# Attention beside a mixture of experts: tags in one load, and a tile's up-weight pieces split in two places

## The chip, the cores and the metric

One core of a Trainium2 chip runs the whole program in one launch. The metric is the time of an execution on the device in microseconds; lower is better. Engines are called TensorE (PE in the profile, PEld for its weight loads), VectorE (DVE), ScalarE (ACT), GpSimd (POOL) and SyncE (SP, which here only issues transfers and waits). An ending q (DVEq, SPq) marks the instruction queue of an engine: register work, waits, and the issuing of transfers.

## What is computed

The inputs are 2 x 1024 rows of 512 numbers. After a layer norm the output is the sum of three parts:

```python
xn = _layernorm(x, axis=-1)
x = x + attention(xn) + experts(xn)        # both read the same xn

# attention: 16 heads of 32, rotary embedding over the heads, causal softmax, scaled by 512 ** -0.5, projection
# experts: 8 of them, the best 2 per row, their weights normalised to sum 1
gate_up = jnp.einsum('th,eoh->eto', x, w1)          # w1: 8 x 704 x 512
g, u = jnp.split(gate_up, 2, axis=-1)
act = jax.nn.silu(g) * u
expert_out = jnp.einsum('eti,ehi->eth', act, w2)    # w2: 8 x 512 x 352
out = jnp.einsum('eth,te->th', expert_out, combine)
```

## The kernel before

**Stages.** `project_qkv` (up to about 110 us) normalises the rows, projects them, chooses two experts for each row and writes to memory. `attend` runs 16 rounds, a pair of heads each, of about 19.5 us; meanwhile it sorts the rows by expert: `route` gives each (row, choice) a place, and POOL scatters the row there by an indirect transfer into `routed` (32 transfers, in rounds 0 to 8, counted by `scattered`). `experts`, from about 562 us on, first does the second half of the output projection (8 steps, `LATE`), and then works through `SLOT_TILES` = 39 tiles of 128 sorted rows, each belonging to one expert.

**A routed row** has 514 numbers: 512 of xn, then its tag: the row of the output to which it belongs (an integer in the bits of a float), and the weight of the choice. In `acc` the output is gathered, by an indirect transfer that adds.

**A tile i of `experts`** takes these steps, and most buffers are double (r = i % 2):
- ScalarE loads `rows` (L816), three tiles ahead. TensorE turns them (`turn_rows`, L932) into `turn_ps`. ScalarE rounds them to `rows_hi` (L822), VectorE takes the rest as `rows_lo` (L888): two numbers of reduced precision stand for one float.
- The up weights are split in the same way, in DK = 4 pieces of 128 x 704: ScalarE casts `w1_hi` (`up_weights_high`, L826), VectorE subtracts (`up_weights_low`, L895, `w1_lo`, called w_lo in the trace). `w1_done` counts the pieces.
- TensorE forms the products `up(i, r, j)` in two halves, j = 0 for g and j = 1 for u, 12 products each: for each of the four pieces hi x hi, hi x lo, lo x hi (L940, L941, L942).
- ScalarE takes the silu of g (`gated`, L851), VectorE multiplies by u (`hidden`, L911), TensorE turns that (`turn_hidden`, L950), VectorE copies it (`hidden_t`, L881, L882), and TensorE multiplies it by w2 (`down_product`, L958, six passes).
- ScalarE scales the result by the weight in the tag into `y` (L839). POOL adds `y` to `acc` by the row numbers in the tag (L802), after the accumulate before it has landed (`added`), since two tiles can hold the same row.

**The order on each engine** is written out by hand, one `tile` function each, and each engine works its queue in order:
- TensorE in tile i: down(i-2), up half 0 of i, turn_hidden(i-1), turn_rows(i+1), up half 1 of i. Before half 0 it waits for all four pieces of tile i.
- ScalarE in tile i: y(i-2), the front two casts of tile i+1, silu(i), rows_hi(i+1), the rear two casts of i+1, and the load of rows(i+3).
- VectorE in tile i: the front two subtractions of tile i+1, hidden_t(i-1), rows_lo(i+1), the rear two subtractions of i+1, hidden(i).
- POOL in tile i: waits until y(i) is there and the accumulate i-1 has landed; a small `carrier` instruction; the accumulate i; then the load of the tag of tile i+1 (`load_tag`, L792), one piece of 8 bytes per partition. `y`(i) waits for that tag (`tag_in`).

Each engine reads a tile's place in the ring of weights from memory into a register (`slot_at`, `value_load`, L739). `run_tiles` writes tiles 0 to 3 and the last one (for ScalarE the last three) with constant addresses; those between are a loop of two tiles each, with addresses in registers. SP keeps a ring of three experts' weights (2.1 MB each, L757 to L759): an expert's weights are overwritten once `y_read` shows that its last tile is through.

## Time and profile before

| | us |
|---|---|
| median of 3 runs | 934.96 |
| the 3 runs | 934.89, 943.35, 934.96 |
| the profiled execution: its time | 937.0 |
| its span, first to last instruction | 935.1 |
| TensorE busy in the span | 829.9 (89%) |
| VectorE busy | 515.4 (55%) |
| ScalarE busy | 395.0 (42%) |
| GpSimd busy | 272.6 (29%) |

Times in rows are microseconds from the first instruction of the profiled execution, unless they are marked ns. A row of the timeline is: start, length, engine, line, operation, what is written <- what is read, shape, count, and in brackets how long the engine stood idle before it and what released it. Rows of neighbouring instructions of one kind are merged: their count is behind the x, their length that of the group. A share of busy time says nothing about what bounds a stage; the rows below are taken from the stage that the change touches.

### The profile page before, as it was taken

What the parts mean: (1) busy time and instruction counts of PE and PEld (TensorE: products, weight loads), DVE (VectorE), ACT (ScalarE), POOL (GpSimd) and SP (SyncE); (2) the same over time, 40 slices, a digit from 0 to 9 for tenths busy, and PEclk for the clock granted to TensorE, in tenths of its full rate; (3) what the DMA queues carried; (4) which work ended last, traced back from release to release, by engine and by line L of the source; (5) the groups of instructions that cost most, each with busy time, mean ns of one, the idle gap of its engine ahead of it and who ended that gap; (6) DMA issues with size and microseconds to landing.
All of it is one profiled execution on the core that took longest, in us unless ns stands there. A gap on an engine that the chain in (4) does not pass through costs nothing. (4 is left out here: it accounts for less than half of the span.)

```text
span 935.1 us, 13836 instructions
## 1 busy us (share of the span) xinstructions
PE 829.9 (89%) x3973; PEld 561.9 (60%) x3974; DVE 515.4 (55%) x1334; ACT 395.0 (42%) x779; POOL 272.6 (29%) x352
## 2 busy tenths in 40 slices
PE   3889999289989999999999999798989889899990
PEld 3678988254545555555554444576767667677760
DVE  5983453584566666666674021664656546666640
ACT  3321221014545555555655400454545545455630
POOL 3781000405132342423331510032323323333330
PEclk9999999758899999999999999998999999999995
DMA  9386596867356576676730138434454453633336
GB/s 318 142 262 206 202 312 203 250 164 227 97 155 165 175 182 165 182 189 178 196 100 14 41 103 275 161 68 137 73 151 120 100 149 67 160 68 67 68 35 200
DMA packets 76717, 143.21 MB, mean 153 GB/s; under 512 B 12928, under 2 KB 26752, under 8 KB 76608
## 3 DMA queue, kind: packets, MB, share of 16 engines
q10 hardware_dynamic: 29056, 58.28, 22.7%
q1 hardware_dynamic: 38192, 65.68, 22.7%
q0 software_dynamic: 9424, 18.69, 9.9%
q8 instruction: 22, 0.36, 0.2%
q14 instruction: 23, 0.19, 0.1%
HBM read 81.21 MB, written 61.15 MB: 152 GB/s over the span
## 5 line engine op out<-in xcount | busy, mean ns | idle before, releaser
L1342 ACT ACTIVATE probs<-scores_t 128x512 f32<-128x512 f32 (+3 forms) x384 | 163.8, 492 | 148.0 <-PE scores_t L1469 136.1
L895 DVE TENSOR_TENSOR w_lo<-w,w_hi 128x704 fp32r<-128x704 f32 x156 | 131.6, 884 | 121.3 <-ACT w_hi L826 115.7
L1446 PE MATMUL maxima<-k_stack,q_stack 96*128 96x512 f32 (+3 forms) x384 | 142.4, 391 | 15.2 <-DMA q_stack<-qk_hi 9.1
L1489 PE MATMUL o_acc<-probs,v_ones 128*64 128x512 f32 (+3 forms) x768 | 149.1, 511 | 0.0
L1469 PE MATMUL scores_t<-q_stack,k_stack 98*128 98x512 f32 (+3 forms) x384 | 138.3, 385 | 7.3 <-DMA q_stack<-row_lo 5.2
L1376 DVE TENSOR_REDUCE mx<-maxima 128x1 f32<-128x512 f32 x128 | 88.2, 689 | 88.4 <-PE maxima L1446 88.2
L1372 DVE CUSTOM_DVE_ANT_0 masked_scores<-maxima,mask_m 128x128 f32<-128x128 f32 (+3 forms) x256 | 121.6, 485 | 24.2 <-PE maxima L1446 21.1
L958 PE MATMUL down<-w,hidden_t 128*128 (+1 forms) x234 | 114.8, 628 | 20.7 <-DVE hidden_t L882 20.7
L826 ACT CAST w_hi<-w 128x704 fp32r x156 | 114.0, 782 | 34.7 <-issue 33.5
L940 PE MATMUL gu<-w_hi,rows_hi 128*128 128x352 f32 x312 | 120.6, 386 | 5.3 <-DVE rows_lo L888 4.0
L1469 PEld LDWEIGHTS scores_t<-q_stack,k_stack 98*128 98x128 f32 x384 | 73.5, 194 | 69.3 <-issue 42.1
L941 PE MATMUL gu<-w_lo,rows_hi 128*128 128x352 f32 x312 | 101.8, 326 | 0.0
L942 PE MATMUL gu<-w_hi,rows_lo 128*128 128x352 f32 x312 | 101.5, 325 | 0.0
L1446 PEld LDWEIGHTS maxima<-k_stack,q_stack 96*128 96x128 f32 x384 | 77.4, 203 | 36.0 <-DVE mx L1376 10.0
L1287 POOL TENSOR_SCALAR_AFFINE_SELECT probs<-probs 128x256 f32<-128x256 f32 x120 | 48.4, 406 | 145.3 <-ACT probs L1342 143.5
L1489 PEld LDWEIGHTS o_acc<-probs,v_ones 128*64 128x64 f32 x768 | 47.7, 139 | 64.7 <-issue 39.6
L839 ACT ACTIVATE y<-down,tag 128x512 f32<-128x512 f32 x39 | 26.8, 688 | 140.9 <-DMA tag<-routed 90.2
L958 PEld LDWEIGHTS down<-w,hidden_t 128*128 128x128 f32 (+1 forms) x234 | 44.0, 199 | 66.9 <-issue 66.6
L801 POOL TENSOR_TENSOR carrier_y<-ident 128x1 f32<-128x1 f32 x39 | 7.3, 188 | 242.2 <-ACT y L839 242.2
L802 POOL DMA_INDIRECT acc<-y,tag x39 | 63.9, 1639 | 16.9 <-issue 16.9
L940 PEld LDWEIGHTS gu<-w_hi,rows_hi 128*128 128x128 f32 x312 | 59.4, 190 | 15.6 <-DVE w_lo L895 6.3
L941 PEld LDWEIGHTS gu<-w_lo,rows_hi 128*128 128x128 f32 x312 | 59.5, 191 | 9.2 <-issue 9.2
(158 smaller groups left out, 1175.7 us busy)
## 6 DMA issues: line engine op xcount, KB each, us to landing
w<-in_w_t SPq DMA_DIRECT2D x8, 1408.0 KB, 6.4
routed<-blank_row ACTq DMA_DIRECT2D x20, 514.0 KB, 7.2
rows<-routed ACTq DMA_DIRECT2D x39, 256.0 KB, 3.6
qk_hi<-st_hi SPq DMA_DIRECT2D x32, 256.0 KB, 4.7
qk_lo<-st_lo SPq DMA_DIRECT2D x32, 256.0 KB, 6.1
q_stack<-qk_hi ACTq DMA_DIRECT2D x32, 256.0 KB, 4.0
k_stack<-qk_hi ACTq DMA_DIRECT2D x26, 256.0 KB, 4.7
v_all<-o_t SPq DMA_DIRECT2D x4, 1536.0 KB, 5.7
```

What stands on the lines that cost most here:

```text
L826: nc.scalar.copy(w1_hi[r][:, k, :], w1_rows(slot, k)).then_inc(w1_hi_done, 1)
L895: nc.vector.tensor_tensor(w1_lo[r][:, k, :], w1_rows(slot, k), as_f32(w1_hi[r][:, k, :]), ALU.subtract).then_inc(w1_done, 1)
L940: nc.tensor.matmul(out, hi, w1_hi[r][:, k, cols], start=(k == 0), stop=False)
L941: nc.tensor.matmul(out, hi, w1_lo[r][:, k, cols], start=False, stop=False)
L942: last = nc.tensor.matmul(out, lo, w1_hi[r][:, k, cols], start=False, stop=(k == DK - 1))
L958: last = nc.tensor.matmul(down[r][:], hidden_t[r][0:n, k, :], w2[0:n, bass.ds(e, 1), k, :].rearrange("p o n -> p (o n)"), start=(k == 0), ...
L1342: nc.scalar.activation(probs[:, k % PR, h, 0:w], scores_t[e % RING][:, 0:w], ACT.Exp).then_inc(exp_done, 1)
L1372: nc.vector.tensor_tensor_reduce(out=masked_scores[bank][:, 0:w], in0=scores, in1=mask_m[:, CH - w:CH], scale=1.0, scalar=NEG, op0=ALU.add ...
L1376: nc.vector.tensor_reduce(to, scores, AX.X, ALU.max).then_inc(m_free, 1)
L1446: nc.tensor.matmul(mb[at % RING][:, 0:w], q_st[i][0:3 * HD, h, t * P:(t + 1) * P], k_st[i][0:3 * HD, h, c * CH:c * CH + w], start=True, st ...
L1469: last = nc.tensor.matmul(out[:, 0:w], k_st[i][0:STACK, h, j * P:(j + 1) * P], q_st[i][0:STACK, h, t0:t0 + w], start=True, stop=not diag)
L1489: last = nc.tensor.matmul(o_acc[c][2 * HD * h:2 * HD * (h + 1), CH - w:CH], v_st[i][:, j, h:h + 2, :].rearrange("p o d -> p (o d)"), probs ...
```

## The change

The tags of all 39 tiles are loaded by one transfer, issued by SP in round 9 of `attend` into a tile `tags` that lives through the program (39 x 2 numbers per partition, so 4,992 pieces of 8 bytes). SP waits for `scattered` before it. `load_tag`, `tag_in` and the carrier instruction go; POOL copies the row numbers of the next tile into `row_index`, by an instruction in the place of the carrier, since the indirect transfer takes its addresses from there. In `experts` the split of the up weights moves: ScalarE casts the front two pieces of tile i+1 behind rows_hi(i+1), and the rear two as the first thing in tile i+1. VectorE subtracts all four pieces of tile i as the first thing in tile i. TensorE waits for each piece on its own within half 0. In the projection steps ahead of tile 0, its casts, its subtractions and its announcement each move one step up.

```diff
@@ -695,9 +695,9 @@
         hidden = [m.sbuf(f"hidden{r}", [P, I], F32) for r in range(2)]
         hidden_t = [m.sbuf(f"hidden_t{r}", [P, len(I_TILES), P], F32) for r in range(2)]
         y = m.sbuf("y", [P, 2, D], F32)
-        tag = m.sbuf("tag", [P, 2, XW - D], F32)
+        tags = keep["tags"]
         warm = m.sbuf("warm", [P, 1], F32)
-        carrier = m.sbuf("carrier_y", [P, 2], F32)
+        row_index = m.sbuf("row_index", [P, 2], F32)
         gu = [[m.psum(f"gu{r}{j}", [P, CH]) for j in range(2)] for r in range(2)]
         turn_ps, hid_ps = m.psum("turn_ps", [P, CH]), m.psum("hid_ps", [P, CH])
         down = [m.psum(f"down{r}", [P, CH]) for r in range(2)]
@@ -707,7 +707,6 @@
         expert_ready = m.sem("expert_ready")
         proj_full, res_done = m.sem("proj_full"), m.sem("res_done")
         rows_in = [m.sem(f"rows_in{r}") for r in range(2)]
-        tag_in = [m.sem(f"tag_in{r}") for r in range(2)]
         acc_started = keep["acc_started"]
         added, stored = m.sem("added"), m.sem("stored")
         carried, warmed = m.sem("carried"), m.sem("silu_table_warmed")
@@ -787,24 +786,21 @@
             pool.wait_ge(pool_chain, 1)
             nc.gpsimd.affine_select(out=ident[:], in_=ident[:], compare_op=ALU.not_equal, fill=1.0, base=0,
                                     pattern=[[-1, P]], channel_multiplier=1).then_inc(ident_done, 1)
-            def load_tag(i, r):
-
-                pool.dma_start(tag[:, r:r + 1, :], in_rows[bass.ds(i, 1), :, D:XW].rearrange("a p d -> p a d")).then_inc(tag_in[r], 16)
+            def tag_of(i):
+                return tags[:, bass.ds(i, 1), 0:1].rearrange("p o n -> p (o n)")
+
+            nc.gpsimd.tensor_copy(row_index[:, 0:1], tag_of(0)).then_inc(carried, 1)
 
             def tile(i, r, half):
                 pool.wait_ge(y_read, i + 2)
                 if past(i, 1):
                     pool.wait_ge(added, i * 16)
-                if past(i, 2):
-                    pool.wait_ge(carried, i - 1)
-
-                nc.gpsimd.tensor_tensor(carrier[:, r:r + 1], ident[:, 0:1], ident[:, 0:1], ALU.mult).then_inc(carried, 1)
+                pool.wait_ge(carried, i + 1)
+                after = i if isinstance(i, int) and i == SLOT_TILES - 1 else i + 1
+                nc.gpsimd.tensor_copy(row_index[:, 1 - r:2 - r], tag_of(after)).then_inc(carried, 1)
                 pool.indirect_dma_start(out=scratch["acc"], out_offset=bass.IndirectOffsetOnAxis(
-                    ap=tag[:, r, 0:1].bitcast(U32), axis=0), in_=y[:, r, :], in_offset=None, compute_op=ALU.add).then_inc(added, 16)
-                if not (isinstance(i, int) and i == SLOT_TILES - 1):
-                    load_tag(i + 1, 1 - r)
-
-            load_tag(0, 0)
+                    ap=row_index[:, r:r + 1].bitcast(U32), axis=0), in_=y[:, r, :], in_offset=None, compute_op=ALU.add).then_inc(added, 16)
+
             pool.wait_ge(acc_started, 16 * NT)
             run_tiles(pool, tile)
             pool.wait_ge(added, 16 * SLOT_TILES)
@@ -833,25 +829,23 @@
 
             def y_to_sbuf(i, r, half):
                 act.wait_ge(y_full, i + 1)
-                act.wait_ge(tag_in[r], half * 16 + 16)
                 if not early(i):
                     act.wait_ge(added, i * 16 - 16)
-                nc.scalar.activation(y[:, r, :], down[r][:], ACT.Copy, scale=tag[:, r, 1:2]).then_inc(y_read, 1)
+                nc.scalar.activation(y[:, r, :], down[r][:], ACT.Copy, scale=tags[:, bass.ds(i, 1), 1:2].rearrange("p o n -> p (o n)")).then_inc(y_read, 1)
 
             def tile(i, r, half):
+                if past(i, 1):
+                    up_weights_high(r, slot_at(act, i), range(DK // 2, DK))
                 if past(i, 2):
                     y_to_sbuf(i - 2, r, half - 1)
                 more = not (isinstance(i, int) and i == SLOT_TILES - 1)
-                if more:
-                    slot = await_up_weights(i + 1)
-                    up_weights_high(1 - r, slot, range(0, DK // 2))
                 act.wait_ge(gu_full, i * 2 + 1)
                 if past(i, 1):
                     act.wait_ge(hidden_done, i)
                 nc.scalar.activation(gated[:], gu[r][0][:, 0:I], ACT.Silu).then_inc(silu_done, 1)
                 if more:
                     rows_to_sbuf(i + 1, 1 - r)
-                    up_weights_high(1 - r, slot, range(DK // 2, DK))
+                    up_weights_high(1 - r, await_up_weights(i + 1), range(0, DK // 2))
                 if not (isinstance(i, int) and i + 3 >= SLOT_TILES):
                     load_rows(i + 3, 1 - r)
 
@@ -861,8 +855,9 @@
             act.wait_ge(ident_done, 1)
             nc.scalar.activation(warm[:], ident[:, 0:1], ACT.Silu).then_inc(warmed, 1)
             for a in range(LATE):
+                if a == LATE - 2:
+                    up_weights_high(0, await_up_weights(0), range(DK))
                 if a == LATE - 1:
-                    up_weights_high(0, await_up_weights(0), range(DK))
                     rows_to_sbuf(0, 0)
                     load_rows(2, 0)
                 at = EARLY + a
@@ -896,14 +891,12 @@
 
             def tile(i, r, half):
                 more = not (isinstance(i, int) and i == SLOT_TILES - 1)
-                if more:
-                    slot = slot_at(dve, i + 1)
-                    up_weights_low(i + 1, 1 - r, slot, range(0, DK // 2))
+                if past(i, 1):
+                    up_weights_low(i, r, slot_at(dve, i), range(DK))
                 if not (isinstance(i, int) and i == 0):
                     hidden_to_sbuf(i - 1, 1 - r)
                 if more:
                     rows_low(i + 1, 1 - r)
-                    up_weights_low(i + 1, 1 - r, slot, range(DK // 2, DK))
                 dve.wait_ge(silu_done, i + 1)
                 dve.wait_ge(gu_full, i * 2 + 2)
                 if not early(i):
@@ -916,7 +909,7 @@
 
                 nc.vector.tensor_tensor(o_t[:, :, at * P:(at + 1) * P], gu[a % 2][a // 2 % 2][:].rearrange("p (g t) -> p g t", t=P),
                                         res[:, at, :].rearrange("p (g t) -> p g t", t=P), ALU.add).then_inc(res_done, 1)
-                if a == LATE - 2:
+                if a == LATE - 3:
                     up_weights_low(0, 0, slot_at(dve, 0), range(DK))
             rows_low(0, 0)
             run_tiles(dve, tile)
@@ -935,6 +928,8 @@
             def up(i, r, j):
                 out = gu[r][j][:, 0:I]
                 for k in range(DK):
+                    if j == 0:
+                        pe.wait_ge(w1_done, i * DK + (k + 1))
                     hi, lo = (t[r][:, k * P:(k + 1) * P] for t in (rows_hi, rows_lo))
                     cols = slice(j * I, (j + 1) * I)
                     nc.tensor.matmul(out, hi, w1_hi[r][:, k, cols], start=(k == 0), stop=False)
@@ -970,7 +965,6 @@
                     pe.wait_ge(hidden_done, i - 1)
                 else:
                     pe.wait_ge(res_done, LATE)
-                pe.wait_ge(w1_done, i * DK + DK)
                 up(i, r, 0)
                 if past(i, 1):
                     turn_hidden(i - 1, 1 - r)
@@ -987,7 +981,7 @@
                 at = EARLY + a
                 if a >= 4:
                     pe.wait_ge(res_done, a - 3)
-                if a == LATE - 2:
+                if a == LATE - 3:
                     announce_tile(0)
                 if a == LATE - 1:
                     turn_rows(0, 0, 0)
@@ -1082,7 +1076,7 @@
 
         proj_banks = scores_t + mb
 
-        scattered = m.sem("scattered")
+        scattered, tags_in = m.sem("scattered"), m.sem("tags_in")
         w_proj_in = m.sem("w_proj_in")
         numbered, weighted = m.sem("rows_numbered"), m.sem("rows_weighted")
         masked = m.sem("probs_masked")
@@ -1202,6 +1196,8 @@
             for n in range(ROUNDS):
                 if n == BIAS_ROUND - 1:
                     sp.dma_start(bp[:], b_proj.partition_broadcast(P)).then_inc(bp_in, 16)
+                    sp.wait_ge(scattered, 16 * TOPK * NT)
+                    sp.dma_start(keep["tags"][:], scratch["routed"][0:SLOT_TILES * P, D:XW].rearrange("(a p) d -> p a d", p=P)).then_inc(tags_in, 16)
                 if n:
                     sort_out(n - 1, NC - 1)
                 if n % PAIRS == 1 and n > PAIRS:
@@ -1214,6 +1210,7 @@
                 if n % PAIRS == 0 and n:
                     store_shares(n // PAIRS - 1)
             sort_out(ROUNDS - 1, NC - 1)
+            sp.wait_ge(tags_in, 16)
             load_totals(SPANS - 1)
             store_shares(SPANS - 1)
             spread_shares(SPANS - 1)
@@ -1556,6 +1553,7 @@
             "x_rows": m.sbuf("x_rows", [P, NT, XW], F32),
             "expert_end": m.sbuf("expert_end", [1, E], I32),
             "tile_slot": m.sbuf("tile_slot", [1, SLOT_TILES], I32),
+            "tags": m.sbuf("tags", [P, SLOT_TILES, XW - D], F32),
             "acc_started": m.sem("acc_started"),
         }
         with ExitStack() as until_attended:
```

## Rows read from the trace of the kernel before

**Rows 1.** The page's chain that ended last, by line: shares of the span.

```profile
PE down L958 9%; DMA tag<-routed 5%; PE gu L942 3%; PE gu L940 3%; PE gu L941 3%; ACT w_hi L826 1%; POOL acc L802 1%; DVE hidden_t L881 1%; PE turn_ps L932 1%; ACT y L839 1%; PE hid_ps L950 0%; DVE hidden_t L882 0%; ACTq L739 0%; POOL carrier_y L801 0%; ACTq L816 0%
```

**Rows 2.** By stretch: length, busy PE, PEld, DVE, ACT, POOL, clock, DMA share, GB/s.

```profile
604.14:902.44 298.30, 278.38 (x1371) 215.21 (x1369) 178.49 (x295) 159.93 (x257) 88.38 (x110) 0.98 0.44 99
820.00:900.00 80.00, 78.88 (x396) 61.27 (x395) 53.42 (x88) 47.16 (x76) 26.90 (x33) 1.00 0.37 66
700.00:740.00 40.00, 36.24 (x185) 28.38 (x184) 23.67 (x40) 21.61 (x35) 12.22 (x15) 1.00 0.50 119
```

**Rows 3.** The table of waits from 660 to 935 us: total, times, longest.

```profile
ACT y L839 <- DMA tag<-routed: 75.1, 18, 6.6
```

**Rows 4.** Transfers issued at 752 to 754 us; last, us to landing.

```profile
acc<-y,tag POOLq DMA_INDIRECT x1, 9.1
tag<-routed POOLq DMA_DIRECT2D x1, 1.0 KB, 8.4
```

**Rows 5.** The timeline of TensorE and ScalarE, 752 to 766 us.

```profile
752.16 0.49 PE L950 MATMUL hid_ps<-ident,hidden 128*128 128x128 f32 x3
...
754.91 2.74 PE L958 MATMUL down<-w,hidden_t 128*128 x6
...
759.42 0.49 PE L950 MATMUL hid_ps<-ident,hidden 128*128 128x128 f32 x3
...
761.68 0.69 ACT L839 ACTIVATE y<-down,tag 128x512 f32<-128x512 f32 x1 [6.62 <-DMA tag<-routed]
...
765.85 4.27 PE L958 MATMUL down<-w,hidden_t 128*128 x6 [3.60 <-DVE hidden_t L882]
```

**Rows 6.** The timeline at the stage's start, and one row near its end.

```profile
590.11 3.30 DVE L895 TENSOR_TENSOR w_lo<-w,w_hi 128x704 fp32r<-128x704 f32 x4 [2.64 <-ACT w_hi L826]
...
594.66 0.66 PE L940 MATMUL gu<-w_hi,rows_hi 128*128 128x352 f32 x1 [4.04 <-DVE rows_lo L888]
...
600.29 1.69 DVE L895 TENSOR_TENSOR w_lo<-w,w_hi 128x704 fp32r<-128x704 f32 x2
...
602.13 0.40 PE L940 MATMUL gu<-w_hi,rows_hi 128*128 128x352 f32 x1 [1.29 <-DVE w_lo L895]
...
602.37 0.32 PE L941 MATMUL gu<-w_lo,rows_hi 128*128 128x352 f32 x1
...
602.53 0.32 PE L942 MATMUL gu<-w_hi,rows_lo 128*128 128x352 f32 x1
...
604.14 0.49 PE L950 MATMUL hid_ps<-ident,hidden 128*128 128x128 f32 x3
...
604.33 0.46 ACT L851 ACTIVATE gated<-gu 128x352 f32<-128x352 f32 x1 [1.37 <-PE gu L942]
...
902.44 0.49 PE L950 MATMUL hid_ps<-ident,hidden 128*128 128x128 f32 x3
```

**Rows 7.** VectorE's queue in two tiles: ns, first and last start.

```profile
L910 DVEq EVENT_SEMAPHORE  x1: 21/21/21, 868.8 to 868.8; - x1
...
L894 DVEq ALU_OP  x1: 45/45/45, 870.0 to 870.0; - x1
...
L910 DVEq ALU_OP  x1: 40/40/40, 876.2 to 876.2; - x1
...
L739 DVEq TENSOR_LOAD <-tile_slot x1: 312/312/312, 876.4 to 876.4; - x1
...
L894 DVEq ALU_OP  x1: 45/45/45, 877.2 to 877.2; - x1
```

**Rows 8.** The timeline of ScalarE at the end.

```profile
914.40 0.69 ACT L839 ACTIVATE y<-down,tag 128x512 f32<-128x512 f32 x1 [6.08 <-DMA tag<-routed]
```

**Rows 9.** Timeline of round 9; POOL's queue from 562.6 to 569.2 us.

```profile
396.71 0.43 SPq L1204 DMA_DIRECT2D bp_early<-in_b_proj  x1
...
411.36 2.36 POOL L1272 TENSOR_TENSOR o_t<-o_t,share_rows 128x1024 f32<-128x1024 f32 x1 [9.33 <-DMA share_rows<-shares_all]
...
q0 software_dynamic: 32, 0.00, 0.8%
```

## The prediction

> **What bounds the kernel now.** I read the views from the whole to the single tile. The chain of waits comes first [rows 1]: of what ended last the reader sees products of TensorE (L958, L940 to L942), and one transfer, the load of the tags, with 5% of the span. It stands only in the expert stage. There TensorE is busy for 278.38 of 298.30 us, VectorE for 178.49; in the stretch from 820 to 900 us, in which no weights come in, TensorE is busy for 78.88 of 80 (the columns are those of the page: busy time and count by engine, then the granted clock) [rows 2]. So the stage is near TensorE's own pace, and loses time only where something else is late. The table of waits says what: ScalarE's `y` waits 75.1 us in 18 waits for the tag [rows 3].
>
> Two landings explain why. The tag of tile i+1 is issued by POOL just behind the indirect accumulate of tile i. While weights stream in, the accumulate lands after 9.1 us and the tag, issued some 1 us later, after 8.4 [rows 4]. The tag thus lands together with the accumulate ahead of it, and `y`(i) in effect waits for the accumulate i-1, though its buffer needs only i-2.
>
> The timeline shows what that costs [rows 5]. The hidden transposes (L950, I call their start H, one per tile) at 752.16 and 759.42 are 7.26 apart: this tile waits for nothing, and 7.25 is TensorE's own period. In the next one `y` starts at 761.68 after 6.62 us of waiting for the tag; ScalarE's casts are queued behind it, VectorE's subtractions and its copy of `hidden_t` behind these, and the down products begin at 765.85, 3.60 late, and take 4.27 instead of 2.74, which is what a lowered clock looks like. From the first H at 604.14 to the one at 902.44 [rows 2, 6] there are 37 periods in 298.3 us: 8.06 each. TensorE's own would be 37 x 7.25 = 268.3, so 30 us are there to be won.
>
> **The change, part by part.** *The tags.* POOL loses 39 loads from the loop, `y` its wait for them. Even a slow accumulate (9.1) is now met by `y` two tiles later, some 16 us on: the stalls under weight traffic go. POOL's copy of the row index takes the place of the carrier instruction one for one, and ScalarE's scale read from a register address is a few tens of ns on an engine with slack; I put 0 for both. What is late next is the question, and the answer is in the other part.
>
> *The order of VectorE.* Before, two of a tile's four subtractions came ahead of the `hidden` product of the tile before. Now all four come behind it, and `hidden`(i) needs the second half of tile i's up products. TensorE, in turn, needs the fourth subtraction for the last three products of the first half of tile i+1. That closes a loop between two engines, which I add up from H:
> - The down products start at H + 2.75 (754.91 - 752.16) [rows 5], directly behind the last up product. An engine released by the product just before H started at H + 0.19 (604.33 against 604.14) [rows 6]. So `hidden` is released at 2.94; with the register arithmetic of its last wait, 3.04.
> - VectorE's queue may go on only then. In the loop it does the L910 step and, behind it, loads the tile's slot into a register, adjusts and asserts it, and computes two wait values. From L910 to the last of these (L894) the two kinds of tile take 877.2 - 876.2 = 1.0 and 870.0 - 868.8 = 1.2 us; the longer one crosses the loop's edge [rows 7]. The `hidden` product starts within a tenth of the former, the subtraction within two tenths of the latter, so I take 1.0 and 1.3 from start to start. Before, all this lay beside running subtractions.
> - Four subtractions in a row took 3.30 [rows 6].
> - TensorE's first product started 0.15 after the subtraction that released it (602.13, against 600.29 + 1.69), the second 0.24 after that, and then the step is 0.16: to the next H, 0.15 + 0.24 + 0.16 + 0.16 = 0.71 [rows 6].
>
> The sum is 3.04 + 1.0 + 3.30 + 0.71 = 8.05 or, with 1.3, 8.35; the mean is 8.20. That is above 7.25, so VectorE's chain binds in every tile. TensorE's waits for the single pieces don't help: a subtraction follows each 0.8 us, three products take some 0.5.
>
> Tiles 4 to 37 are in the register-addressed loop (the last H follows tile 38): 34 x 8.20 = 278.8. The two before them and the last one have constant addresses, without the edge and most of the arithmetic; I estimate 0.5 less for the two (7.7, so 15.4) and 0.3 less for the last (7.9). Together 302.1 against 298.3: +3.8 us. The removed stalls (30) are given back by a wait in every tile, some 34 in all. Bounds of the queue's part: at least 0.43 us, a back-to-back start with all register work hidden; at most 1.6, should the loop's edge come in every tile and the waits need more arithmetic. These give 7.5 and 8.65 per tile, or -24 and +16 for the loop tiles.
>
> The Trainium skill (DMA: Bandwidth & Descriptors, "Latency and other measured facts") gives a floor of about 600 ns for a register load from memory. The row here shows 0.31 us for this load on VectorE [rows 7], so the measurement decides; by the page each loop tile would be 0.29 longer, 34 x 0.29 = 10 us in all, and the kernel slower by over 1%.
>
> *ScalarE.* The rear casts move behind the tile's edge. Front pieces are ready long before `hidden` is done, and the rear ones at about H + 5.3, while the fourth subtraction starts near H + 6.5. Hidden, by about a microsecond; cost 0.
>
> *Start of the stage.* TensorE waits 4.04 us before tile 0 (594.66) [rows 6]. Casts and subtractions of tile 0 move one projection step up; about 2 us of this wait stay, because VectorE's last two additions now lie behind the four subtractions and ScalarE's `rows_hi` behind one of them. But tile 1 now has its 3.30 us of subtractions behind `hidden`(0), which costs 1 to 1.5. Net -1.0; bounds -3 and +1.
>
> *End.* The last `y` (914.40) waited 6.08 us for its tag, which is the upper bound of a gain [rows 8]. The last accumulate still waits for the one before it, which lands nearly with the tag. I take -1.0, and 0 as the other bound.
>
> *Round 9.* SP gets 4,992 pieces of 8 bytes behind `bp_early` (396.71). The wait for `scattered` is long met, as 32 scatters end in round 8. Queued behind are the outputs of round 8, the shares, and the next rows. The shares are wanted: POOL stood 9.33 us for them until 411.36, and its masks follow [rows 9]. Price of a piece: the first tag's 128 pieces took 0.8% of 16 engines over 6.6 us, 0.84 us of engine time. Its 32 packets may be a merged count, or a quarter of the pieces; so 4,992 pieces are 33 to 131 us of engine time, 2 to 8 us on all 16, and done by some 400 to 408 us. I take +0.5; bounds 0 and +5.
>
> The Trainium skill (same page, "Measured (HBM to SBUF)") puts a floor of about 10.5 ns to a packet; as a rule for the whole transfer it would make 52 us of this load, against 2 to 8 by the row. By it the shares would come some 40 us late.
>
> **Sum.** +3.8 - 1.0 - 1.0 + 0.5 = +2.3 us. The profiled execution took 937.0 (span 935.1), so 939.3 by it. The median of the runs is 934.96, 2.0 below it; the forecast for the median is 937.3.
>
> **Rivals.** What can be told from no change here is about 1%, 9.3 us.
> - *The register work is partly hidden* (0.10). If it costs VectorE 0.6 and not 1.0 to 1.3, the period is 7.65; 34 x 7.65 + 23.3 = 283.4, -14.9; with -1.5 for the rest 918.6. For it: the load alone is only 0.31. Against: the steps around it, which fill the rest.
> - *TensorE's pace* (0.08). Queue work fully hidden: with 0.43 the period is 7.48, near TensorE's 7.25; 37 x 7.48 = 276.8, -21.5 - 1.5: 912. Against: the queue can't pass its own wait.
> - *A dearer queue* (0.09), slower: at 1.4 us on the mean, with more arithmetic behind the released wait than the L910 step shows, 8.45 x 34 + 23.3 = 310.6, +12.3 - 1.5: 946. From 0.2 us per tile over my sum it makes the kernel slower by 1%. The skill's floor for a register load, above, would lead there too.
> - *The tag transfer in round 9* (0.05), slower: where it holds the queue past 408, each further us comes on TensorE through POOL's scaling and masks. From 17 us of transfer the kernel is slower by 1%; at 20 it is 949. The packet floor cited above, taken piece by piece, would give 977.
> - *The clock* (0.06), slower: TensorE stands for about 0.9 us in each tile, in pieces of 0.15 to 0.3. The 3.60 us wait brought the clock down [rows 5]. If such small ones lower it by a tenth, the 3.3 us of products in the loop cost 0.33 more, 12 us in all: 949. Against: from 700 to 740 us TensorE was busy for 36.24 of 40 and was granted 1.00 [rows 2].
>
> **Numbers.** My forecast has 0.62, with a range of its own of 930 to 944. With the dearer queue whole, and the slower part of the partly hidden one, some 0.8 are in: 920 to 947. Faster by over 1%: the two fast rivals less their nearer part, 0.17. Slower by over 1%: the three slow ones, 0.20. Within: 0.63.
>
> **What would show it.** Right: no wait of `y` for a transfer; VectorE's sequence `hidden`, then about 1.1 us later four `w_lo` without a gap; TensorE waiting for `w_lo` three or four times in each tile; H to H of 8.0 to 8.4, the same with and without weight traffic; granted clock near 1.0. Wrong: a period of 7.3 to 7.6, or waits for `y` again; POOL's wait for `share_rows` near 411 us grown beyond 10 us; a period of over 8.5.

## The result and the profile after

The changed kernel takes 935.33 us (median of 20 runs, 926.54 to 941.71), the kernel before 939.76 beside it (20 runs, 930.85 to 944.01). The ratio is 0.9946, with a 95% interval of 0.992 to 0.9973: half a per cent or 5 us faster, small but clear of the noise, where 2.3 us slower was forecast. The ratio goes by the fast executions alone, so it is not quite the quotient of the two medians. The median of 934.96 known before was thus some 5 us below what more runs gave. The profiled execution took 933.14 us, with a span of 931.2 (935.1 before).

The chain that ended last, by line, from the page of the kernel after. Against [rows 1] the transfer of the tag is gone, and the first entry is now VectorE's subtraction.

```profile
DVE w_lo L890 9%; PE down L953 4%; PE gu L935 3%; ACT w_hi L822 2%; PE gu L937 2%; PE gu L936 2%; ACTq L738 2%; PE turn_ps L925 2%; PE hid_ps L945 1%; PE gu L989 1%; ACTq L812 1%; DVEq L738 0%; PEld gu L989 0%; ACTq L822 0%; DVEq L890 0%
```

The same stretch as the first row of [rows 2], first H to last H, in the kernel after (length, busy time of PE, PEld, DVE, ACT and POOL, clock, DMA share, GB/s):

```profile
602.91:899.64 296.73, 292.58 (x1371) 209.17 (x1370) 189.89 (x296) 171.31 (x259) 79.52 (x74) 1.00 0.44 99
```

The 37 periods now take 296.73 us instead of 298.30: 8.02 each instead of 8.06. The busy time of TensorE is 292.58 us, though the same products took 278.38 before. So this share can't be read as work done. In the record a product lasts 0.32 us and the next starts 0.16 behind it, so a short break between two products lies under the first of them and counts as busy; the table of waits shows the standing. Waits from 603 to 900 us in the kernel after (total, times, longest):

```profile
PEld gu L935 <- DVE w_lo L890: 46.4, 129, 1.2
...
ACT y L834 <- PE down L953: 32.0, 36, 1.2
...
DVE w_lo L890 <- issue: 14.3, 23, 1.0
...
ACT y L834 <- DMA acc<-y,row_index: 0.2, 1, 0.2
```

`y` waited 75.1 us for its tag in [rows 3] (79.6 from the first H to the last); now it waits 0.2 for a transfer, and for down products, which is where it should wait. In its place TensorE waits 129 times for a subtraction. This is the trade that the prediction described. Two tiles in a stretch without weight traffic, TensorE first, then VectorE:

```profile
844.06 0.49 PE L945 MATMUL hid_ps<-ident,hidden 128*128 128x128 f32 x3
...
851.59 0.43 PE L935 MATMUL gu<-w_hi,rows_hi 128*128 128x352 f32 x1
...
852.18 0.49 PE L945 MATMUL hid_ps<-ident,hidden 128*128 128x128 f32 x3
...
859.93 0.49 PE L945 MATMUL hid_ps<-ident,hidden 128*128 128x128 f32 x3
```

```profile
846.93 0.52 DVE L904 TENSOR_TENSOR hidden<-gu,gated 128x352 f32<-128x352 f32 x1 [0.50 <-PE gu L937]
848.24 3.30 DVE L890 TENSOR_TENSOR w_lo<-w,w_hi 128x704 fp32r<-128x704 f32 x4 [0.78 <-issue]
...
855.05 0.53 DVE L904 TENSOR_TENSOR hidden<-gu,gated 128x352 f32<-128x352 f32 x1 [0.50 <-PE gu L937]
855.98 3.30 DVE L890 TENSOR_TENSOR w_lo<-w,w_hi 128x704 fp32r<-128x704 f32 x4 [0.41 <-issue]
```

H to H is 8.12 and 7.75 in turn. `hidden` starts 2.87 behind H, the subtractions 1.31 or 0.93 behind `hidden`, they take 3.30, and TensorE is at the next H 0.64 or 0.65 later. "issue" behind the bracket means that nothing the profile shows held the engine: it is the queue's own work.

### The profile page after: what moved, and what is told of

Its sections match the earlier page's. It is cut to its first block and busy times, and to the rows that moved or that the text cites. A ratio compares the mean times of both kernels' runs of the same rounds, so it can differ in the third digit from the quotient of the medians.

```text
span 931.2 us, 13974 instructions
## 1 busy us (share of the span) xinstructions
PE 844.5 (91%) x3973; PEld 555.4 (60%) x3974; DVE 525.6 (56%) x1334; ACT 405.0 (43%) x779; POOL 261.5 (28%) x314
## 3 DMA queue, kind: packets, MB, share of 16 engines
q0 software_dynamic: 8176, 18.65, 10.5%
## 5 line engine op out<-in xcount | busy, mean ns | idle before, releaser
L890 DVE TENSOR_TENSOR w_lo<-w,w_hi 128x704 fp32r<-128x704 f32 x156 | 128.6, 887 | 27.0 <-issue 14.5
L935 PE MATMUL gu<-w_hi,rows_hi 128*128 128x352 f32 x312 | 123.5, 396 | 8.1 <-DVE w_lo L890 2.3
L953 PE MATMUL down<-w,hidden_t 128*128 (+1 forms) x234 | 106.9, 593 | 0.8 <-DVE hidden_t L877 0.8
L800 POOL COPY row_index<-tags 128x1 f32 (+1 forms) x39 | 21.0, 539 | 257.6 <-ACT y L834 206.8
L1486 PEld LDWEIGHTS o_acc<-probs,v_ones 128*64 128x64 f32 x768 | 47.4, 138 | 64.9 <-issue 39.6
L280 ACT ACTIVATE st_hi<-bank,small 128x512 fp32r<-128x512 f32 x32 | 21.9, 687 | 101.9 <-PE bank L537 101.9
L801 POOL DMA_INDIRECT acc<-y,row_index x39 | 63.1, 1618 | 9.5 <-issue 8.4
```

The lines of the kernel that those rows point to most:

```text
L890: nc.vector.tensor_tensor(w1_lo[r][:, k, :], w1_rows(slot, k), as_f32(w1_hi[r][:, k, :]), ALU.subtract).then_inc(w1_done, 1)
L935: nc.tensor.matmul(out, hi, w1_hi[r][:, k, cols], start=(k == 0), stop=False)
L953: last = nc.tensor.matmul(down[r][:], hidden_t[r][0:n, k, :], w2[0:n, bass.ds(e, 1), k, :].rearrange("p o n -> p (o n)"), start=(k == 0), ...
L1486: last = nc.tensor.matmul(o_acc[c][2 * HD * h:2 * HD * (h + 1), CH - w:CH], v_st[i][:, j, h:h + 2, :].rearrange("p o d -> p (o d)"), probs ...
```

## The experiments

Diffs are against the changed kernel unless said otherwise. H is the start of the hidden transposes, as in the prediction; "the loop" is the 37 periods from the first H to the last; "the start" runs from the first product of the projection to the first H (before 41.70 us, after 41.16), "the tail" from the last H to the end of the span (32.66 and 31.56). All kernels compute the whole output.

**Each half alone.** In `tags_only` the tags come in one load, and the order of the split and of the start is that of the kernel before:

```diff
 # ScalarE, tile i
-                if past(i, 1):
-                    up_weights_high(r, slot_at(act, i), range(DK // 2, DK))
...
+                if more:
+                    slot = await_up_weights(i + 1)
+                    up_weights_high(1 - r, slot, range(0, DK // 2))
...
-                    up_weights_high(1 - r, await_up_weights(i + 1), range(0, DK // 2))
+                    up_weights_high(1 - r, slot, range(DK // 2, DK))
 # VectorE, tile i
-                if past(i, 1):
-                    up_weights_low(i, r, slot_at(dve, i), range(DK))
+                if more:
+                    slot = slot_at(dve, i + 1)
+                    up_weights_low(i + 1, 1 - r, slot, range(0, DK // 2))
...
+                    up_weights_low(i + 1, 1 - r, slot, range(DK // 2, DK))
 # TensorE
-                    if j == 0:
-                        pe.wait_ge(w1_done, i * DK + (k + 1))
...
+                pe.wait_ge(w1_done, i * DK + DK)
```

> The tags in one load, the split of the up weights and the start as before. Theory A (the changed kernel's period of 7.75 and 8.11 us per tile is set by the loop hidden -> VectorE's queue -> four subtractions -> products, which the new order of the split closed): with the order of before the loop is open, nothing waits for a tag, and the period falls to TensorE's own 7.25 to 7.35 in all tiles, with and without weight traffic: 37 periods in 268 to 272 us against 298.3 before and 296.7 after. With 3 to 4 us lost in round 10 the kernel takes 0.970 to 0.976 of before. Rival B (the memory traffic itself, not the tag's place, makes the long tiles of before, through rows or accumulates): five or so tiles above 9 us remain, ratio 0.985 to 1.0.

Measured: 906.89 us (4 runs), ratio 0.9701, interval 0.9638 to 0.9765. The loop of this kernel, and three Hs of it:

```profile
602.94:870.53 267.59, 267.59 (x1371) 211.74 (x1370) 178.46 (x295) 160.03 (x257) 66.98 (x74) 1.00 0.49 110
```

```profile
805.51 0.49 PE L945 MATMUL hid_ps<-ident,hidden 128*128 128x128 f32 x3
...
812.72 0.49 PE L945 MATMUL hid_ps<-ident,hidden 128*128 128x128 f32 x3
...
819.95 0.49 PE L945 MATMUL hid_ps<-ident,hidden 128*128 128x128 f32 x3
```

TensorE has no break: 267.59 of 267.59 us busy, a period of 7.23, just below the expected 268 to 272. The one edit gives the whole 30 us that the prediction counted as there to be won. The table of waits of this kernel from 603 to 871 us still has the accumulate, late but met two tiles on:

```profile
ACT y L834 <- DMA acc<-y,row_index: 48.8, 18, 2.7
```

`split_only` is the opposite: the kernel before (its `load_tag`, carrier and `tag_in`) with the changed order of split and start:

```diff
-        tags = keep["tags"]
+        tag = m.sbuf("tag", [P, 2, XW - D], F32)
...
-                pool.wait_ge(carried, i + 1)
-                after = i if isinstance(i, int) and i == SLOT_TILES - 1 else i + 1
-                nc.gpsimd.tensor_copy(row_index[:, 1 - r:2 - r], tag_of(after)).then_inc(carried, 1)
+                if past(i, 2):
+                    pool.wait_ge(carried, i - 1)
...
+                nc.gpsimd.tensor_tensor(carrier[:, r:r + 1], ident[:, 0:1], ident[:, 0:1], ALU.mult).then_inc(carried, 1)
...
+                    load_tag(i + 1, 1 - r)
...
+                act.wait_ge(tag_in[r], half * 16 + 16)
```

> The new split and start, the tags per tile as before. Theory A: undisturbed tiles take 7.75 and 8.11 in turns, and where weights come in, y waits for its tag as before, but with less harm (y has about 2 us of slack in a period of 8), so some five tiles of 9 to 10.5 us: 37 periods in 300 to 308 us, ratio to before 1.00 to 1.01; round 10 takes its usual 19.5 to 20.5 us. Rival B: the split is the part that brings the gain (by TensorE's waits for single pieces) and the tags bring little: ratio below 0.995.

Measured: 934.5 us (12 runs), ratio 0.9953 (0.992 to 0.9985), the same as the whole change. Its loop, and two rows of its waits from 603 to 902 us:

```profile
603.54:901.54 298.00, 293.68 (x1370) 209.51 (x1369) 189.72 (x296) 169.03 (x259) 98.85 (x110) 1.00 0.45 99
```

```profile
ACT y L839 <- DMA tag<-routed: 51.8, 20, 4.9
PEld gu L940 <- DVE w_lo L895: 48.0, 131, 1.1
```

I had expected tiles of 9 to 10.5 us to stay here, and they did not. `y` still waits 51.8 us for tags, but the wait no longer reaches VectorE: its subtractions wait 10.4 us in all for ScalarE's casts, against 111.2 in the kernel before and 9.8 in the kernel after. Two reasons are at hand, and no run parts them: the period of 8.05 set by VectorE leaves `y` more time, and the rear casts of the tile now stand ahead of `y` on ScalarE, the front ones far behind it. So the two halves don't add. The new order alone removes the long tiles (up to 13.69 us from H to H before), and pays for it with 0.8 us in every tile; the tags alone remove them and pay nothing. Together they cost what the dearer one costs.

**The price of VectorE's queue.** In `slot_early` the four subtractions of tile i+1 stand behind `hidden`(i) in the same tile, and the slot is loaded ahead of the waits of `hidden`, so the register work is done while VectorE waits for TensorE:

```diff
-                if past(i, 1):
-                    up_weights_low(i, r, slot_at(dve, i), range(DK))
...
+                if more:
+                    slot = slot_at(dve, i + 1)
                 dve.wait_ge(silu_done, i + 1)
                 dve.wait_ge(gu_full, i * 2 + 2)
...
+                if more:
+                    up_weights_low(i + 1, 1 - r, slot, range(DK))
```

> The changed kernel, with VectorE's four subtractions of tile i+1 written at the end of tile i (the same order of its instructions, only the loop's edge moves) and with the load of the tile's slot into a register ahead of hidden's wait. Theory A: 0.93 and 1.31 us from hidden to the first subtraction become 0.5 to 0.6 in both kinds of tile; the period falls to 7.3 to 7.45 everywhere, 37 periods in 271 to 276 us, ratio to before 0.972 to 0.98. Rival C (the period is set elsewhere, by ScalarE's casts or by TensorE's own register waits): the gap closes, but the period stays above 7.7, ratio 0.99 or more.

Measured: 911.88 us (4 runs), ratio 0.9738 (0.968 to 0.9797). Its loop, and VectorE at one `hidden`:

```profile
601.77:873.27 271.50, 271.45 (x1371) 212.02 (x1369) 186.57 (x296) 171.42 (x259) 64.63 (x74) 1.00 0.48 109
```

```profile
854.24 0.53 DVE L904 TENSOR_TENSOR hidden<-gu,gated 128x352 f32<-128x352 f32 x1 [0.51 <-PE gu L939]
854.68 3.29 DVE L890 TENSOR_TENSOR w_lo<-w,w_hi 128x704 fp32r<-128x704 f32 x4
```

From `hidden` to the first subtraction it is 0.44 us, back to back, instead of 0.93 to 1.31; the mean of these is 0.68 more, and 37 x 0.68 is the 25 us that the loop loses of its 296.73. The term is real, and it decides the kernel.

`edge_moved` has the same place for the subtractions, but the slot is loaded there, behind `hidden`:

```diff
-                if past(i, 1):
-                    up_weights_low(i, r, slot_at(dve, i), range(DK))
...
+                if more:
+                    up_weights_low(i + 1, 1 - r, slot_at(dve, i + 1), range(DK))
```

> The changed kernel, with VectorE's slot load and four subtractions of tile i+1 written at the end of tile i: the same order of its instructions, the slot load still behind hidden, only the loop's edge moves away from between them. If the edge costs the 0.38 us by which the gaps of 1.31 and 0.93 us differ, both gaps become 0.93 and the period 7.75 in every tile (37 periods in 288 to 291 us); if the difference is the register arithmetic of one kind of tile, the periods stay 7.75 and 8.11 in turns. With slot_early this parts the cost of the edge from that of the load.

Measured: 928.45 us in one run; its span is 926.7, and its loop 292.79 (7.91 a tile). Two tiles of its VectorE:

```profile
842.80 0.52 DVE L902 TENSOR_TENSOR hidden<-gu,gated 128x352 f32<-128x352 f32 x1 [0.50 <-PE gu L937]
843.74 3.30 DVE L890 TENSOR_TENSOR w_lo<-w,w_hi 128x704 fp32r<-128x704 f32 x4 [0.42 <-issue]
...
850.65 0.52 DVE L902 TENSOR_TENSOR hidden<-gu,gated 128x352 f32<-128x352 f32 x1 [0.60 <-PE gu L937]
851.58 3.30 DVE L890 TENSOR_TENSOR w_lo<-w,w_hi 128x704 fp32r<-128x704 f32 x4 [0.41 <-issue]
```

Both kinds of tile now have the short gap (0.94 and 0.93). In every second tile `hidden` itself starts 0.09 later (2.96 behind H instead of 2.87), so the period there is 7.84, and the loop is a little above the 288 to 291 expected. In the gap the loop's edge is thus worth 1.31 - 0.93 = 0.38 in every second tile, and the slot's load with its arithmetic the other 0.93 - 0.44 = 0.49 in each.

**The single waits.** In `one_wait` TensorE waits for all four pieces at once, as before, under the changed order of VectorE:

```diff
-                    if j == 0:
-                        pe.wait_ge(w1_done, i * DK + (k + 1))
...
+                pe.wait_ge(w1_done, i * DK + DK)
```

> The changed kernel, with TensorE waiting for all four pieces ahead of its first product of a tile, as before. Theory A: the loop then holds all twelve products of the first half behind the fourth subtraction, instead of three: nine steps of 0.16 us more, 1.4 us per tile, periods of 9.2 and 9.55, 37 periods in 345 to 350 us. If the separate waits are worth nothing (as the prediction said in passing), it stays near 297.

Measured: 1013.78 us in one run, span 1011.8, the loop 378.70 (10.2 a tile). Two first products of it, and a stretch:

```profile
802.33 0.43 PE L933 MATMUL gu<-w_hi,rows_hi 128*128 128x352 f32 x1 [1.75 <-DVE w_lo L890]
...
811.96 0.43 PE L933 MATMUL gu<-w_hi,rows_hi 128*128 128x352 f32 x1 [2.11 <-DVE w_lo L890]
```

```profile
800.00:900.00 100.00, 80.66 (x367) 63.40 (x366) 49.91 (x79) 44.57 (x68) 22.43 (x20) 0.91 0.35 72
```

The 12 products of the half now begin behind the fourth subtraction instead of the last 3 of them. That alone gave my expectation of some 348 us. The rest is the clock, and it comes in every second tile, as these two show, from H to H:

```profile
794.91:804.36 9.45, 7.70 (x39) 5.88 (x38) 5.13 (x8) 4.56 (x7) 2.06 (x2) 0.97 0.19 45
804.36:815.23 10.87, 8.76 (x39) 6.91 (x38) 5.13 (x8) 4.66 (x7) 2.41 (x2) 0.87 0.37 58
```

The first takes what was expected (9.2 to 9.55); in the second the products of the first half start 0.29 us apart (812.59, 812.88, 813.17) instead of 0.16. Over the loop, with a stall of 1.7 to 2.1 us in each tile, the granted clock is 0.91. In the changed kernel the weight loads of TensorE wait three to four times in a tile, for 0.36 us on the mean (46.4 / 129) and 1.2 at most. Part of that lies beside the product ahead; the loop is 29.1 us longer than that of `tags_only`, 0.23 for each wait. The clock stays at 1.00.

**The load of the tags.** In `tags_moved` it is issued behind the rows of the next round, and no longer ahead of the shares:

```diff
                 if n == BIAS_ROUND - 1:
                     sp.dma_start(bp[:], b_proj.partition_broadcast(P)).then_inc(bp_in, 16)
-                    sp.wait_ge(scattered, 16 * TOPK * NT)
-                    sp.dma_start(keep["tags"][:], ...).then_inc(tags_in, 16)
...
                     rows(n + 1)
+                if n == BIAS_ROUND - 1:
+                    sp.wait_ge(scattered, 16 * TOPK * NT)
+                    sp.dma_start(keep["tags"][:], ...).then_inc(tags_in, 16)
```

> The changed kernel, with SP's load of the tags issued behind the rows of round 10 instead of 7 us ahead of the share rows. Theory A (the load of 4,992 pieces lands after 7.7 us, delays the share rows, POOL's scaling and the masks, and made the step from the rows of round 10 to those of round 11 23.7 us long against 20.5 before): that step is 19.5 to 20.5 again, and the kernel takes 3 us less than the changed kernel, ratio to before 0.989 to 0.993. Rival D (that step was long by chance, the clock or other traffic): the step is short or long regardless, and the ratio stays at 0.9946.

Measured: 934.57 us (12 runs), ratio 0.9965 (0.993 to 0.9999), not to be told from the change's 0.9946; the 3 us expected didn't come. What can be told stands in the timelines. The round in question, from the first rows of round 10 to those of round 11 on SP's queue, in the kernel after, with the load of the tags and POOL's wait for the shares (11.14 us against 9.33 in [rows 9]):

```profile
392.94 0.43 SPq L1200 DMA_DIRECT2D tags<-routed  x1
...
407.89 0.52 SPq L1155 DMA_DIRECT2D q_stack<-row_hi  x1
...
408.53 2.36 POOL L1269 TENSOR_TENSOR o_t<-o_t,share_rows 128x1024 f32<-128x1024 f32 x1 [11.14 <-DMA share_rows<-shares_all]
...
431.61 0.52 SPq L1155 DMA_DIRECT2D q_stack<-row_hi  x1
```

The step is 23.72 us here, 20.50 before. What TensorE waited for in it, first after, then before:

```profile
411.30 1.72 PE L1486 MATMUL o_acc<-probs,v_ones 128*64 128x512 f32 x8 [0.79 <-POOL probs L1284]
...
414.85 0.50 PE L1466 MATMUL scores_t<-q_stack,k_stack 98*128 98x512 f32 x1 [1.82 <-DMA q_stack<-row_lo]
```

```profile
417.76 0.50 PE L1469 MATMUL scores_t<-q_stack,k_stack 98*128 98x512 f32 x1 [0.96 <-DMA q_stack<-row_lo]
```

The masks cost 0.79 and the rows of the next round 0.86 more than before, 1.65 together. The other 1.6 of the step's 3.2 go with the clock: it was 0.93 over this step, and 1.00 in that of all other kernels named here. In the kernels with the load in its place the two waits cost 1.65 (after), 1.46 (`tags_only`), 1.38 (`edge_moved`), 0.92 (`one_wait`) and 0 (`slot_early`), 1.1 on the mean, and the step is 23.72, 22.03, 21.95, 21.48 and 20.48. Without it there (before, `split_only`, `tags_moved`, `tags_and_start`) no product waits for the masks, and the step is 20.45 to 20.95 (`tags_moved`, whose wait for the rows is 1.40). POOL's wait for the shares parts the two groups cleanly: 9.92 to 11.14 us in the five, 9.23 to 9.33 in the four. So the load costs some 1.1 us, in single executions 0 to 1.7, and more than half of it comes by the rows and not by the masks.

`tags_fourfold` makes the cost large: three more loads of the same kind behind the first.

```diff
+        spare = m.sbuf("spare", [P, 3, SLOT_TILES, XW - D], F32)
...
+                    for copy in range(3):
+                        sp.dma_start(spare[:, copy], ...).then_inc(tags_in, 16)
...
-            sp.wait_ge(tags_in, 16)
+            sp.wait_ge(tags_in, 64)
```

> The changed kernel, with the load of the tags issued four times in round 9 (three copies into a spare tile). If the load's traffic is what lengthened the step from the rows of round 10 to those of round 11 (23.7 us in the changed kernel, 22.0 in tags_only, 20.5 in slot_early, 20.5 before), four loads land after some 25 us instead of 7.7, the share rows come up to 18 us later, and the step grows to 35 us or more. If queue and engines pass share rows and rows by, or the load takes far less than its landing says, the step stays at 20 to 24 us.

Measured: 945.88 us in one run, span 944.0. Its SP queue, from the rows of round 9 on, and POOL's wait:

```profile
387.18 0.52 SPq L1156 DMA_DIRECT2D q_stack<-row_hi  x1
...
392.15 19.69 SPq L1203 DMA_DIRECT2D spare<-routed  x3
...
423.84 0.59 SPq L1156 DMA_DIRECT2D q_stack<-row_hi  x1
...
424.59 2.34 POOL L1272 TENSOR_TENSOR o_t<-o_t,share_rows 128x1024 f32<-128x1024 f32 x1 [27.21 <-DMA share_rows<-shares_all]
...
445.79 0.52 SPq L1156 DMA_DIRECT2D q_stack<-row_hi  x1
```

The chain that the prediction named is there to be seen: SP can't issue the next rows for 19.69 us, the shares come late (27.21), and the masks hold TensorE, as its waits from 380 to 430 us show:

```profile
PE o_acc L1489 <- POOL probs L1287: 16.9, 1, 16.9
```

The delay falls one step earlier than expected: since SP is held before it can issue the rows of round 10, the step from the rows of round 9 to those of round 10 takes 36.66 (19.49 in the kernel after), and the one from there to round 11, of which the expectation spoke, 21.95 (423.84 to 445.79). The two together take 58.61, against 43.21 after. One load is mostly covered by the slack of the round, four are not. A single load lands 7.7 us after its issue, by the list of transfers of the kernel after; below it, the traffic of SP's queue in `tags_fourfold` from 405 to 411 us (packets, MB, share of 16 engines):

```profile
tags<-routed SPq DMA_DIRECT2D x1, 39.0 KB, 7.7
...
q1 hardware_dynamic: 3143, 0.03, 33.9%
```

That is 0.339 x 16 x 6 us / 3,143 = 10.4 ns of engine time for a piece. At this price three loads would take 9.7 us of all engines (an estimate: 3 x 4,992 x 10.4 ns / 16), and SP was held for 19.69. The other queue's packets had a share of 77.2% in the same stretch, which is likely what makes the difference; no run shows the load without them.

**The best version tried.** `tags_and_start` is `tags_only` with the new start of the stage and the load moved as in `tags_moved`:

```diff
 # against tags_only; the load also moved behind rows(n + 1)
-                if a == LATE - 1:
+                if a == LATE - 2:
                     up_weights_high(0, await_up_weights(0), range(DK))
+                if a == LATE - 1:
...
-                if a == LATE - 2:
+                if a == LATE - 3:
                     up_weights_low(0, 0, slot_at(dve, 0), range(DK))
...
-                if a == LATE - 2:
+                if a == LATE - 3:
                     announce_tile(0)
```

> The best of the parts: tags in one load, the split's order as before, the casts and subtractions of tile 0 one projection step up as in the changed kernel, and the load of the tags behind the rows of round 10. From the first projection product to the first hidden transposes it took 41.7 us with the old start (before, tags_only), 39.1 to 39.6 with the new start (slot_early, split_only): so 38.5 to 39.5 here, since tile 1 isn't held by its subtractions; 37 periods in 267.6 us; ratio to before 0.965 to 0.970, against 0.970 of tags_only.

Measured: 901.79 us (896.24 to 906.54, 4 runs) beside 938.12, ratio 0.96 (0.9523 to 0.9676), a little better than expected. It beats both kernels; against `tags_only` the intervals overlap. Its start takes 39.53 us against 41.68 there, in an execution that was granted a lower clock in its first microseconds, and the loop runs at TensorE's pace. The first product of tile 0, and most of the loop:

```profile
595.97 0.43 PE L936 MATMUL gu<-w_hi,rows_hi 128*128 128x352 f32 x1 [1.94 <-DVE rows_lo L884]
```

```profile
601.00:868.00 267.00, 266.07 (x1364) 211.85 (x1365) 179.70 (x296) 160.76 (x258) 67.74 (x72) 1.00 0.49 110
```

## Why the prediction was right and wrong

The mechanism was the forecast one. VectorE's chain closes a loop with TensorE, in every tile, with and without weight traffic, and gives back nearly all that the tags free: 267.59 us became 296.73. The sign was wrong by the size of one term. That the forecast of 937.3 us lies only 2.0 above the measured median is luck: it starts from a median before that was 4.8 too low, and the shift between the kernels was missed by about 7 us.

**The loop: 302.1 predicted, 296.7 measured.** This is the step that failed: the period of 8.20, a sum of small terms of which most were taken too large. In quiet stretches the two kinds took 8.12 and 7.75 where 8.35 and 8.05 stood, 0.27 less on the mean. By the terms of the sum:
- From H to `hidden` 2.87, not 3.04. The down products start 2.67 behind H in most tiles here and not 2.75, and `hidden` 0.20 behind them, so there is no room for a further 0.10 of arithmetic.
- From `hidden` to the first subtraction 1.31 and 0.93, where 1.3 and 1.0 stood. This, the uncertain term, was nearly exact.
- Four subtractions 3.30, as said.
- From their end to the next H 0.64 and 0.65, not 0.71: the released product started 0.05 behind the subtraction instead of 0.15, and what follows took 0.59 instead of 0.56.

34 x 0.27 is 9.2 us too much. One thing that I had left out worked the other way: some tiles take 8.2 to 8.7. The slot's load into a register, on VectorE in the kernel after:

```profile
L738 DVEq TENSOR_LOAD <-tile_slot x39: 300/307/933, 584.4 to 894.9; - x39
L738 DVEq TENSOR_LOAD <-tile_slot x1: 933/933/933, 686.3 to 686.3; - x1
```

The columns are least, median and longest in ns. The load of 933 ns at 686.3 stands between `hidden` and the subtractions of the tile whose first subtraction waited 1.40 us; from H to H that tile took 8.74:

```profile
687.88 3.30 DVE L890 TENSOR_TENSOR w_lo<-w,w_hi 128x704 fp32r<-128x704 f32 x4 [1.40 <-ACT w_hi L822]
```

It is not the weight traffic as such: the weights before it had been issued by 674.5 and had landed, and the DMA engines stood from 683 to 686 us. What goes before each long load is POOL's accumulate:

```profile
683.88 1.55 POOL L801 DMA_INDIRECT acc<-y,row_index  x1 [0.48 <-issue]
```

Five of the seven VectorE loads of over 0.33 us in this loop start 2.2 to 2.7 us behind the start of such an accumulate, the other two 3.4 and 3.8 behind it. The mean excess over 7.93 is 0.09, 3.3 us in 37 periods: about 2.5 of it in the gap before the subtractions, the rest in tiles whose down products start at 2.75. 302.1 - 9.2 + 3.3 = 296.2. The forecast "the same with and without weight traffic" was wrong by this, and its two errors partly cancelled. In `slot_early`, where the load lies beside a wait, all tiles but one (7.69) take 7.24 to 7.42.

**The removed stalls: 30 us, right**, and measured by themselves in `tags_only`: 298.30 - 267.59 = 30.7.

**"TensorE's waits for the single pieces don't help": wrong.** The sentence is true only of the last three products, which set the loop. Taking the waits away made the loop 82 us longer. It bore on no number, since the sum had counted three products behind the last subtraction, but a reader would have dropped the part that keeps this order bearable.

**The start: -1.0 predicted, -0.5 in the profile, -2.2 elsewhere.** TensorE's wait fell from 4.04 to 1.93, as reckoned with "about 2 us stay", and tile 1 took its 1 to 1.5: from the first product of tile 0 to the first H it is 9.36 us here and 7.95 in `tags_and_start`, where the subtractions of tile 1 don't stand behind `hidden`(0). What the sum lacked is the clock behind the wait of 4.04: from 594.66 to 604.14 us the kernel before was granted 0.82, and the stretch took 9.48 instead of some 7.95. All kernels with the new start but `one_wait` were granted 1.00 there, which gives back 1.5: -2.1 + 1.4 - 1.5 = -2.2. The first product of tile 0:

```profile
593.55 0.43 PE L935 MATMUL gu<-w_hi,rows_hi 128*128 128x352 f32 x1 [1.93 <-DVE rows_lo L883]
```

In this execution the gain was hidden by the clock at the start of the stage. A stretch of 2 us there, in the kernel after:

```profile
563.00:565.00 2.00, 2.00 (x4) 0.83 (x3) 0.00 (x0) 0.60 (x2) 0.00 (x0) 0.50 0.93 328
```

TensorE was granted 0.50, which is the lower of its two levels (1.2 GHz), and did 4 products; in the same 2 us of the kernel before it was granted 1.00 and did 6. From 561.75 to 567 us the clock was 0.67 on the mean; from the first product of the projection to that of tile 0 it took 31.80 us, against 30.11 in the executions granted 1.00, so this cost 1.7 us. `tags_moved` (40.86 us for the start) and `tags_and_start` had the same. Four kernels with the new start that were granted 1.00 there took 39.1 to 39.6 us (`split_only`, `slot_early`, `edge_moved`, `tags_fourfold`), the two with the old one 41.70 and 41.68: -2.2, within the bounds of -3 and +1. The fifth, `one_wait`, took 42.51, since its tile 1 waits for all four pieces at once. Why some executions are granted less there stays open.

**The end: -1.0 predicted, -1.1 measured.** `y` of [rows 8] waits for its own product and no longer for its tag:

```profile
908.62 0.69 ACT L834 ACTIVATE y<-down,tags 128x512 f32<-128x512 f32 x1 [3.28 <-PE down L953]
```

**Round 9: +0.5 predicted, about +1.1 measured**, inside the bounds 0 and +5. The masks alone cost 0 to 0.8, as reckoned; the second way, by which the rows of the next round come late, was not in the sum. POOL's wait of 11.14 us was beyond the 10 named as a sign of being wrong, and yet cost little. The load lands 7.7 us after its issue, within the 2 to 8 given, and a piece took 10.4 ns of engine time, within the 6.6 to 26 of the prediction's 33 to 131 us. The packet floor of the Trainium skill (DMA: Bandwidth & Descriptors, "Measured (HBM to SBUF)"), some 10.5 ns and stated there for loads issued by GpSimd, agrees with this as the time of one engine. Read as a price for the whole transfer it gave 52 us, and the load took 7.7, since 16 engines share the pieces. The prediction's 977 and 949 us for a load of 52 and 20 us don't follow one rule either: by the 8 us from which it counts, 52 gives 981. The floor of 600 ns for a register load (same page, "Latency and other measured facts") is not borne out by the median of 307 ns either.

In the two profiles the parts are -0.7 us up to the start of the stage, -0.5, -1.6 and -1.1, which make the 3.9 by which the spans differ; the medians differ by 4.4, and the ratio means 5. With the start and round 9 as the other executions have them it is -1.6 - 2.2 - 1.1 + 1.1 = -3.8. The only thing changed ahead of the stage is the load of round 9, which costs, so the -0.7 is chance in the rounds.

**The rivals.** The dearer queue, the clock and a long transfer did not come. A partly hidden queue was not the cause either: its gap is as said, and what was smaller lay around it. Each rival stood for one large error. The error that came, 0.27 x 34, is made of three small ones (0.17, 0.03 and 0.07), and it is larger than the whole sum of 2.3, so the sign of the forecast had little under it.

## What to carry to other kernels

Draw the loop between two engines before an order is changed: an instruction at the end of a chain (`hidden`) with the work of the next tile queued behind it makes a period out of that work, however idle the engine looks. Register loads and their arithmetic belong ahead of the wait, where they lie beside it, and not behind it (0.5 us a tile here, 0.9 with the loop's edge). Where a change has two parts that each remove the same stall, time each alone: the better half was worth 33 us, the whole 5.

## What the runs showed of the hardware

- A load of one number into a register takes 0.31 us on VectorE in most tiles and up to 0.93 in the kernel after (ScalarE's up to 0.927). The long ones follow POOL's indirect accumulate. In the ten traces, 39 of the 40 VectorE loads that started 2 to 3 us behind the start of an accumulate took over 0.33 us, and none of the 68 that started 4 to 8 us behind it; of TensorE's it was 16 of 18, and none of 36. Why is not shown.
- In one kernel 129 waits of 0.36 us on the mean left the clock at 1.00, in another one stall of about 2 us in each tile of 10 us went with 0.91, mostly in turns of 0.96 to 1.00 in one tile and 0.81 to 0.88 in the next.
- Pieces of 8 bytes took 9.4 to 11.3 ns of engine time each in four stretches of `tags_fourfold`. Several such loads in a row stop the queue that issues them: 19.69 us for three, beside other traffic.
- Rounds of the same code differ by chance. The step of a round in `attend` before the change took 22.40, 24.46 and 23.57 us, after it 21.69, 21.08 and 24.70; the cost of an edit of 1 us can't be read there from one pair of profiles. The granted clock differs too: 0.93 in one step of round 10 and 1.00 in the same step of the other kernels. The kernel after was 4.6 us ahead of the one before at the first rows of round 10 (407.89 against 412.52), and 0.7 at the start of the stage (561.75 against 562.44).
